# The order of sixteen matmuls in four column strips: interleaved across the strips, or one strip after the other

## The reference

```
q = (x @ Wq + bq).reshape(B, N, 16, 16)
k, v = y @ Wk + bk, y @ Wv + bv          # in heads likewise
attn = softmax(einsum('bnhd,bmhd->bhnm', q, k) / 4)
out = einsum('bhnm,bmhd->bnhd', attn, v).reshape(B, N, 256)
h = relu(out @ W1 + b1);  result = h @ W2 + b2
```

## Time and profile before

| | us |
|---|---|
| median of three runs (lowest, highest) | 754.35 (751.45, 757.32) |
| the profiled execution | 754.35 |
| its span, first to last instruction | 752.5 |
| TensorE matmul busy | 615.7 (82%) |
| VectorE / ScalarE / GpSimd busy | 366.9 / 220.6 / 180.9 |
| mean granted clock | 0.926 |

### The profile page before, as it was taken

The page is one execution under the profiler, slowest core; times in us unless marked ns, Lnnn a source line. Parts: engine busy times, 40 slices in busy tenths (PEclk is TensorE's granted clock), DMA queues, the critical chain, the costliest instruction groups (busy, mean ns, idle before and its releaser), DMA issues.

```text
span 752.5 us, 10605 instructions
## 1 busy us (share of the span) xinstructions
PE 615.7 (82%) x3506; PEld 412.2 (55%) x3507; DVE 366.9 (49%) x925; ACT 220.6 (29%) x361; POOL 180.9 (24%) x151
## 2 busy tenths in 40 slices
PE   4968688898878988889968850599899999999992
PEld 3746455586546864557635640355555555555552
DVE  4434648747487485674739748232222222222221
ACT  1232155531456224553145300122212122211210
POOL 2100223002321013210113001323444433344432
PEclk9977799998999999989999965599999999999997
DMA  9900100002000011000170210112222222222221
GB/s 359 414 14 19 56 1 1 3 21 95 17 0 0 21 56 56 0 0 0 37 270 2 85 45 15 29 23 42 42 42 36 41 36 42 42 42 42 35 33 23
DMA packets 20756, 40.27 MB, mean 54 GB/s; under 512 B 3872, under 2 KB 17440, under 8 KB 19456
## 3 DMA queue, kind: packets, MB, share of 16 engines
q1 hardware_dynamic: 8736, 25.16, 8.9%
q0 software_dynamic: 7488, 10.39, 8.5%
q10 hardware_dynamic: 4512, 4.46, 1.8%
HBM read 30.37 MB, written 9.64 MB: 53 GB/s over the span
## 4 chain that ended last, share of the span: by engine, by line
PE 52%; issue 16%; DVE 10%; DMA 8%; ACT 5%; DVEq 4%; POOL 3%; POOLq 1%; ACTq 0%
PE ps L617 26%; PE ps L953 11%; PE ps L621 8%; DMA keep<-normed,row_in 7%; PE ps L968 5%; DVE ring L1136 2%; DVE mx L1132 2%; POOL var_xh L300 1%; PE ps L776 1%; ACT ring L482 1%; DMA out_x<-OT,row_out 1%; DVEq L1143 1%; ACT keep L586 1%; DVEq L1045 1%; PE ps L780 1%
## 5 line engine op out<-in xcount | busy, mean ns | idle before, releaser
L953 PE MATMUL ps<-experts,keep 128*128 x312 | 145.2, 609 | 8.1 <-ACT keep L586 7.8
L1409 DVE SCALAR_TENSOR_TENSOR keep<-keep,row_w,ps 128x512 f32<-128x512 f32 x39 | 29.2, 749 | 152.3 <-ACT keep L590 152.3
L374 POOL DMA_INDIRECT out_x<-OT,row_out x39 | 61.8, 1584 | 147.9 <-DVE row_out L1417 85.9
L953 PEld LDWEIGHTS ps<-experts,keep 128*128 128x128 f32 x312 | 57.0, 193 | 70.8 <-issue 70.4
L617 PE MATMUL ps<-experts,keep 128*128 128x256 f32 (+1 forms) x184 | 73.7, 553 | 4.8 <-DVE experts L1072 1.7
L968 PE MATMUL ps<-experts,keep 128*128 x312 | 73.9, 380 | 2.0 <-DVE keep L1413 2.0
L300 POOL TENSOR_TENSOR var_xh<-var_xh,minus_half 128x4 f32<-128x4 f32 x16 | 16.9, 1058 | 239.4 <-DVE var_xh L1008 239.4
L968 PEld LDWEIGHTS ps<-experts,keep 128*128 128x128 f32 x312 | 59.1, 190 | 26.2 <-issue 20.1
L590 ACT ACTIVATE keep<-ps 128x512 f32<-128x512 f32 x39 | 23.3, 598 | 134.6 <-PE ps L953 134.6
L1132 DVE TENSOR_REDUCE mx<-ps 128x8 f32<-128x1024 f32 x32 | 39.1, 1221 | 48.6 <-PE ps L617 48.6
L313 POOL TENSOR_TENSOR ring<-experts,keep 128x512 f32<-128x512 f32 x32 | 33.2, 1040 | 97.0 <-PE ps L617 97.0
(11 more groups left out here) (209 smaller groups left out, 876.1 us busy)
## 6 DMA issues: line engine op xcount, KB each, us to landing
experts<-in_experts SPq DMA_DIRECT2D x8, 1536.0 KB, 16.4
keep<-in_keep SPq DMA_DIRECT2D x1, 3075.0 KB, 18.8
ring<-in_fold SPq DMA_DIRECT2D x1, 2112.0 KB, 10.5
experts<-in_x SPq DMA_DIRECT2D x4, 512.0 KB, 3.4
experts<-in_ctxT SPq DMA_DIRECT2D x4, 512.0 KB, 3.7
out_x<-X ACTq DMA_DIRECT2D x4, 512.0 KB, 3.1
normed<-XH ACTq DMA_DIRECT2D x4, 512.0 KB, 4.0
experts<-in_ctx SPq DMA_DIRECT2D x4, 384.0 KB, 3.3
```

The source lines that it names most:

```text
L374: pool.indirect_dma_start(out=out_d, out_offset=bass.IndirectOffsetOnAxis(ap=row_out[u][:, 0:1], axis=0), in_=YO[u], in_offset=None, compu ...
L953: ins = pe.matmul(ps[:, 2 * u + g, :], XIT[u][:, k, :], experts[:, bass.ds(at + (2 * k + g) * INTER, INTER)], start=(k == 0), stop=(k == K ...
L1409: dve.scalar_tensor_tensor(HA[u], HA[u], row_w[u][:, 0:1], ps[:, 2 * u + 1, :], ALU.mult, ALU.mult).then_inc(act_ok, 1)
```

## The change

The loops of `attend1` are turned inside out. Before, all four strips take their first matmul, then all their second, and the same for the sums. Now each strip does its four matmuls in one go, values o = 0 and 1, then sums o = 0 and 1, and then the next strip follows. The instructions, their operands, the accumulation inside each region of PSUM, the waits ahead and the semaphore on the last matmul are the same. (The matmuls now have the helper's line, 617.)

```
-                strip = lambda st: ps[32 * st:32 * st + 32, attend_bank(u), :]
-                for o in range(2):
-                    for st in range(4):
-                        pe.matmul(strip(st)[:, 0:S], V1[:, bb, o, 32 * (4 * t + st):32 * (4 * t + st) + 32], PQ[u % 2][:, 2 * st + o, :],
-                                  start=(o == 0), stop=(o == 1))
-                for o in range(2):
-                    for st in range(4):
-                        ins = pe.matmul(strip(st)[:, S:2 * S], kept("ones_half", 2)[:, o, :], PQ[u % 2][:, 2 * st + o, :],
-                                        start=(o == 0), stop=(o == 1))
+                for st in range(4):
+                    out = ps[32 * st:32 * st + 32, attend_bank(u), :]
+                    mm(out[:, 0:S], [(V1[:, bb, o, 32 * (4 * t + st):32 * (4 * t + st) + 32], PQ[u % 2][:, 2 * st + o, :]) for o in range(2)])
+                    ins = mm(out[:, S:2 * S], [(kept("ones_half", 2)[:, o, :], PQ[u % 2][:, 2 * st + o, :]) for o in range(2)])
                 ins.then_inc(s["ot_ps"], 1)
```

## The result

The changed kernel takes 781.87 us (median of four runs, 780.53 to 781.97) beside 752.93 us for the kernel before in the same comparison (751.45 to 757.32): a ratio of 1.037, 95% interval 1.0338 to 1.0403. Measured again later, beside the experiment `fill2`, it is 1.0385 [1.0354, 1.0415]. It is slower, by 28 to 29 us; 787 was forecast.

The account below looks back on a forecast made before the run. TensorE, busy 615.7 of 752.5 us, was taken as the bound. Three loop turns 28.8, plus last group 9.6, less 5.8 for the clock, gave 32.6 us over 754.35: 787 us, range 771 to 812.

Parts of the forecast that it names:

- The 3 held: In an attend's matmuls: the store in a strip is 3, so a second strip joins 0.57 us in.
- the term of 1.71: Added time of each attend on TensorE: 1.71 us, 54.7 us for 32 attends.
- a deeper strip: Rival: 5 to 9 held, attend 0.7 to 1.4 us longer, waits absorb about half, 768 to 782 us; chance 0.08.
- The walk: Second loop turn, delays followed through TensorE's waits: 9.6 us late at hidden1, 28.8 us for three turns.
- less nothing of note: Attends 6 and 7 back to back at the loop turn's end: 3.42 us added, with nothing notable absorbed.
- The forecast's 9.6: Second loop turn: 9.6 us late at hidden1, before the clock's gain is taken off.
- The last group: Attends after the loop: period 4.87 us in place of 3.66, 9.6 us added in all.
- The clock at S5: From S5 to attend 3 in each turn: granted clock stays at 1.00 where it fell to 0.50.
- The three lose 5.8 now, expected kept: Three loop turns lose 5.8 us to the low clock after S5; the change was to win this back.
- One strip at a time: Rival for the attends: next strip only after the last record starts, 2.37 us more each, 808 to 814 us; chance 0.12.
- Side by side: Rival for the attends: strips overlap as before, attend stays 1.0 us, 0 added; chance 0.12.
- the clock falls in the attends: Case for the attends, where one strip works by itself: granted clock falls there; chance 0.10.

Follow-up runs that it names:

- fill2: Kernel before with dummy matmuls in TensorE's waits around attend 2, plus 2, 3 and 4 more per turn in waits between the attentions: 750.27 us, 0.9943.
- last_only: Kernel before with the strip-by-strip order in the last group alone, the loop left interleaved: 763.0 us beside 756.8, 1.0093.
- fill: Kernel before with 4 dummy matmuls ahead of attend 2 and 8 ahead of S5 in each turn: 752.14 us beside 755.46, 0.9961.
- after_fill: The changed kernel run again with no edit, timed against the kernel before: 784.76 us beside 755.97, 1.0385.
- loop_only: Kernel before with the strip-by-strip order in the loop alone, the last group left interleaved: 779.29 us beside 755.46, 1.0323.
- after_q: The changed kernel with four dummy matmuls ahead of the query of n+1: 776.47 us beside 756.43 for the kernel before, 1.0278.
- runs of two: Kernel before with each strip doing its two value matmuls in a row, then likewise the sums: 755.42 us beside 756.8, 0.997.

## Why the prediction was right, and where it was not

**The course** was the forecast one: with eight pairs of a strip in a row the next strip starts later (0.467 us), the attend is longer (2.39 us in place of 1.01), and the waits absorb only a part of that (of 10.6 us in the second turn, 5.24 arrived). The sign held, and the time lies in the range (787 forecast, 781.87 measured, range 771 to 812). That it came within 5 us is in part luck: the terms that were booked were 11.3 us too high, and 5.3 us that were not booked went the other way.

**The 3 held** were off. No run shows this term, nor the 0.57 and the 1.71 us worked out from it; the earlier trace rows count what had started at two moments and show no store. What the runs showed in its place are starts of the next strip: 0.013 us after the first with four pairs in a row, 0.249 with six, 0.467 with eight, and 0.473 for a pair of strips with eight each. The four fit the estimate of one running pair and three more. So the step between strips is 0.467 us and not 0.57, the attend 2.39 and not 2.7 us, and the term of 1.71 is 1.38. That lies in the rival "a deeper strip", to which I gave 0.08, at its end of 1.4 us; its total of 768 to 782 was reached, but for a partly different reason, since it left the passages between turns out. (The total is also wider than its own words: 22 to 45 us for 32 attends, half of it absorbed, are 11 to 22 us, so 765 to 777.)

**The walk** holds with 1.38 in place of 1.71. Attend 2: 2 x 1.38 - 1.19 = 1.57 (1.43 measured). S5 is as late as shift 4: 1.38 (1.37). The wait of 2.10 is therefore not used up, 0.67 is left; the forecast had it gone. The clock, at 1.00 in place of 0.50, gives back 1.6, then attends 3, 4 and 5 add 1.38 each, T7's wait takes 1.05 away and the longer wait for divide 5 adds 0.48 - 0.22: 3.1 (2.93). Attends 6 and 7 were booked at 3.42 "less nothing of note". They take 254.31 - 250.08 = 4.23 us: unit 7's first strip joins while unit 6's last one runs, so the two together have seven steps of 0.467 and one tail of 0.99, near 4.23, which is 2.33 more than the 1.90 of before. Sum 5.4 (5.24). The forecast's 9.6 less this turn's 1.5 for the clock was 8.1, so 2.9 too much: 1.1 of it are attends 6 and 7, and most of the rest is 1.71 in place of 1.38 ahead of them. Over three turns: 28.8 less 5.8, so 23.0, against 14.4 measured.

**The last group**: 3.16 + 1.38 = 4.54 for the period (4.48), in place of 4.87; 6.9 us in place of 9.6, and 7 by `last_only`. In the changed kernel 0.2 of the 6.9 is the attend that began at 0.50.

**The clock at S5** stayed at 1.00, as forecast, and this turn shows the 1.6. "The three lose 5.8 now, expected kept" was right for TensorE's steps, and `fill` shows that in the kernel before it would have bought only 3, because S6 then waits 0.92 us for VectorE's shift 5. In the changed kernel attend 3 is 1.38 us longer and S6 (235.49) has no wait, so the gain counted in full.

**What the prediction lacked** is the passages between the turns, with the clock in them: 4.1 us in this trace, 6.0 in those of `after_fill` and `loop_only`, and some 7 in the times that `after_q` takes back. It summed falls inside the turns and took the passages as unchanged. Forecast 32.6 = 23.0 + 9.6; measured 26.6 = 14.4 + 6.9 + 4.1 + 1.2.

**The rivals.** One strip at a time is refuted: 2.39 us, and two strips' records start together at 216.16. Strip 1's first record starts there together with strip 0's fifth, and ahead of strip 0's sixth, seventh and eighth, which stand before it in the program. Side by side (0.12) is refuted too: the attend would have stayed at 1.01 us. That the clock falls in the attends (0.10) did not come true either: one attend of 32 began at 0.50, at the end of a stretch that had begun at 411.2 us, ahead of it, and it was 0.23 us longer than the others (2.62 us). What a fall over whole attends would cost no run shows; the query's eight matmuls took 6.67 us at a mean clock of 0.55 and 3.67 at 1.00.

## What to carry to other kernels

Count how many load and matmul pairs of one strip stand in a row. In this kernel's attend (four strips, 32 columns of weights, 128 columns to run over) four pairs, two float32 matmuls, cost nothing measurable (1.05 us in place of 1.01); with six each next strip started 0.249 us later, with eight 0.467. Alternating after four was enough here, and alternating after each matmul was no faster (0.997 [0.9941, 0.9999] for runs of two). For other sizes the trace of the starts has to tell. Before booking time on the engine that bounds, walk it through the waits in order, with each wait's releaser moved as well: the eight attends are 10.6 us longer in a turn (6 x 1.38 + 2.33), and 5.2 arrived. And look at the granted clock behind every wait, not only near the change: in `after_q` one wait of 1.25 us a turn was filled ahead of eight matmuls of 512 columns, and the kernel took some 7 us less.

## What the runs showed of the hardware that was not expected

- **With six and with eight pairs of a strip in a row the next strip started later, with four it did not.** Starts of the second strip: with four pairs in a row 0.013 us after the first, with six 0.249, with eight 0.467; the third strip with two strips that alternate 0.473. That a strip holds four pairs is the estimate that fits these starts. All had 32 columns of weights and 128 columns to run over; other sizes were not run.
- **A stretch at 0.50 and a wait traded places** at the head of a turn. The eleven traces hold two such heads each. In 14 heads the eight 512-column matmuls took 3.68 us, and each time TensorE then stood 1.35 or 1.36 us ahead of the context's transposes; in 8 heads they took 5.17 to 6.56 us, and it never stood there. In the 14 the transposes start when VectorE's normalisation has ended (0.10 us after it at 300.34), so the shorter step ahead of them brought a wait. What decides whether the clock falls there was not settled: the kernel before shows the fall in both heads, runs of two in one.
- **An elementwise step was longer beside GpSimd's work.** The normalisation of the context (1013, now 1008) took 1.96 us before, at 287.38, and 2.68 us in the changed kernel, at 297.66, the same four instructions. GpSimd's second `spread_keys` fell into it now (299.17) and did not before (290.58). All eleven traces agree: in the 14 heads above with a wait of 1.35 us the second `spread_keys` starts 6.34 us after the first of the eight matmuls and the normalisation takes 2.68; in the other 8 it starts 7.8 us after it or later, when the normalisation has ended, and this takes 1.96. So 0.72 of the 1.35 us is this lengthening. That `spread_keys` is its cause was not tried by itself.
